# Attention and quantised FFN on one core: the third input chunk split piece by piece, its query chunk in another bank, and the first FFN group turned in fp32 before its scale is known

## What is computed

```python
x = x + xattn(layernorm(x), ctx)       # 8 heads of 64, 77 context rows per batch, 8 batches of 512 rows
x = x + ffn(layernorm(x))

def ffn(x):
    xq = act_fake_quant(x, clip_x)     # scale = sigmoid(clip) * max|x| / 127, over the WHOLE tensor
    gate, up = xq @ wq(w_gate).T, xq @ wq(w_up).T      # 512 -> 1408, weights quantised by row
    h = act_fake_quant(silu(gate) * up, clip_down)     # again one maximum over the whole tensor
    return h @ wq(w_down).T
```

## Time and profile before

| | |
|---|---|
| median of 3 runs | 535.89 us (535.71 to 536.92) |
| profiled execution, its own time | 535.88 us |
| span of its instructions | 534.1 us |
| PE busy | 524.1 us, 98% of the span |
| DVE busy | 449.2 us, 84% |
| ACT busy | 289.8 us, 54% |
| POOL busy | 230.1 us, 43% |
| granted PE clock | full in all 40 slices |

### The profile page before, as it was taken

One profiled execution on the slowest core, in us unless ns is written; L12 is line 12 of the kernel. 1 busy time (PEld: TensorE's weight loads), 2 busy tenths in 40 slices (PEclk: granted clock), 3 DMA queues, 4 the chain that ended last, 5 costly groups with the idle time before them and its releaser, 6 DMA issues.

```text
span 534.1 us, 7958 instructions
## 1 busy us (share of the span) xinstructions
PE 524.1 (98%) x2717; PEld 354.1 (66%) x2724; DVE 449.2 (84%) x812; ACT 289.8 (54%) x417; POOL 230.1 (43%) x349
## 2 busy tenths in 40 slices
PE   8999999999999999999999999999999999999997
PEld 7888688787888888888778644444444445444444
DVE  4966898989989899898899679998999988777663
ACT  4844656565465655554435745545554543999300
POOL 4396679689596876866453000000000000055332
PEclk9999999999999999999999999999999999999999
DMA  8818465846667565435959964942243020499997
GB/s 311 291 79 293 120 167 188 289 150 217 219 201 243 188 226 182 158 110 174 214 88 337 259 187 190 324 118 41 79 119 91 29 39 19 176 334 207 135 111 122
DMA packets 82941, 93.81 MB, mean 176 GB/s; under 512 B 47085, under 2 KB 50157, under 8 KB 82645
## 3 DMA queue, kind: packets, MB, share of 16 engines
q1 hardware_dynamic: 77877, 84.13, 51.2%
q0 software_dynamic: 4320, 7.87, 9.9%
q10 hardware_dynamic: 704, 1.31, 0.8%
HBM read 47.51 MB, written 37.78 MB: 160 GB/s over the span
## 4 chain that ended last, share of the span: by engine, by line
PE 86%; DVE 6%; POOL 2%; DMA 2%; ACT 1%; issue 1%; SPq 0%; DVEq 0%; ACTq 0%; POOLq 0%
PE QO L613 14%; PE SP L618 14%; PE SP L419 6%; PE QO L335 4%; PE QO L333 4%; PE QO L334 4%; PE SP L665 4%; PE PTP L665 4%; PE QO L665 4%; PE PTP L452 3%; PE WOP L490 2%; PE WOP L492 2%; PE WOP L491 2%; PE MI L492 2%; PE MI L490 2%; PE MI L491 2%
## 5 line engine op out<-in xcount | busy, mean ns | idle before, releaser
L1570 POOL DMA_DIRECT2D out<-n2b x30 | 28.0, 975 | 205.6 <-DVE n2b L1389 205.5
L904 ACT ACTIVATE sil<-QO,fsc 128x512 f32<-128x512 f32 x87 | 59.8, 687 | 71.5 <-PE QO L613 70.9
L613 PE MATMUL QO<-nT,wgu 128*128 128x512 bf16 x340 | 87.3, 379 | 0.1
L618 PE MATMUL SP<-nT,wgu 128*128 128x512 bf16 x340 | 87.3, 379 | 0.0
L1332 DVE SCALAR_TENSOR_TENSOR h<-SP,fsc,sil 128x512 f32<-128x512 f32 x87 | 65.3, 750 | 16.7 <-PE SP L618 13.8
L1471 POOL TENSOR_TENSOR PN<-P,rs 128x512 f32<-128x512 f32 x64 | 44.2, 713 | 43.4 <-DVE rs L988 43.4
L1338 DVE TENSOR_REDUCE hmx<-h 128x1 f32<-128x512 f32 (+1 forms) x89 | 60.1, 679 | 2.9
L618 PEld LDWEIGHTS SP<-nT,wgu 128*128 128x128 bf16 x340 | 33.2, 98 | 40.2 <-DVE h L1332 0.3
L613 PEld LDWEIGHTS QO<-nT,wgu 128*128 128x128 bf16 x340 | 33.2, 98 | 40.2 <-ACT sil L904 0.3
L727 ACT ACTIVATE P<-P,r 128x616 f32<-128x616 f32 x32 | 26.0, 811 | 50.0 <-DVE P L979 50.0
L935 ACT ACTIVATE h<-h,g 128x1536 int8<-128x1536 f32 (+2 forms) x38 | 44.3, 1257 | 0.0
(11 more groups left out here) (230 smaller groups left out, 1204.2 us busy)
## 6 DMA issues: line engine op xcount, KB each, us to landing
xTr<-in_xT SPq DMA_DIRECT2D x8, 1024.0 KB, 7.7
xn<-in_x SPq DMA_DIRECT2D x32, 256.0 KB, 4.2
out<-x SPq DMA_DIRECT2D x32, 256.0 KB, 3.1
n_rows<-n SPq DMA_DIRECT2D x32, 256.0 KB, 2.9
n2b<-n_rows SPq DMA_DIRECT2D x32, 256.0 KB, 3.7
out<-n2b POOLq DMA_DIRECT2D x30, 256.0 KB, 5.6
h_spill<-h SPq DMA_DIRECT2D x2, 2816.0 KB, 8.2
h<-h_spill SPq DMA_DIRECT2D x6, 768.0 KB, 6.7
```

What stands on the lines that cost most here:

```text
L613: mm = e.matmul(QO[:, at:at + 512], wgu_v[:, k, cols(ic)], nT[:, b % 2, :, k, :], start=(k == 0), stop=(k == 3))
L618: mm = e.matmul(SP[:, at:at + 512], wgu_v[:, k, cols(NI + ic)], nT[:, b % 2, :, k, :], start=(k == 0), stop=(k == 3))
L904: e.activation(sil[:, n % SR, :], QO[:, (n % 2) * 512:(n % 2) * 512 + 512], ACT.Silu, scale=fsc[:, ic:ic + 1]).then_inc(silu, 1)
```

## The change

It has two named parts and some small ones.

1. **Third chunk.** `load_xT(2)` is issued ahead of five row loads. `split_hi(b, k)` for `k < 3` waits only for the last product that reads piece `k` (`xT_used`). The piece splits of chunk 2 are interleaved on ACT, DVE and POOL with the end of chunk 1; `q_ahead(2)` writes to the bank `MI` and no longer stands in `QO_USES`; `v_rows(4)` goes ahead of `S(4)`.
2. **First FFN group.** Its fp32 rows are turned on PE while the maximum is still being made; each of the four 128-row pieces `k` of the turned rows then goes PSUM -> int8 -> bf16 (`first_chunk`: 0 and 2 on DVE, 1 and 3 on ACT), and `first_two` multiplies 512 columns at a time. `load_n2(0)`, which brings those rows back from memory, is issued one tile earlier; `top_bank` moves the spreading matmul's output.
3. **Around tile 23.** `wo(23)` is cut: three of its four head pairs ahead of `PV_all(6)`, the fourth behind `PT(28)`; `PV_low(6)` goes ahead of `residual(23)`, and `normed(22)` behind `PT_high(28)`. One small step for tile 31 moves from POOL to DVE and one for tile 30 from DVE to POOL.
4. **Small.** `identB` is gone, the last `h_largest` is one reduce instead of two, the last tile is cut 320 / 192 instead of 256 / 256.

```diff
-        QO_USES += [("q", 1, m) for m in range(4)] + [("v", 4), ("q", 2, 0)]
+        QO_USES += [("q", 1, m) for m in range(4)] + [("v", 4)]
...
         def qo_bank(*use):
+            if use == ("q", 2, 0):
+                return MI[:, :]
...
-        LO_POOL = {0: (), 1: (1, 3), 2: (0, 1)}
-        LO_DVE = {0: (0, 1, 2, 3), 1: (0, 2), 2: (2, 3)}
+        LO_POOL = {0: (), 1: (1, 3), 2: (1, 3)}
+        LO_DVE = {0: (0, 1, 2, 3), 1: (0, 2), 2: (0, 2)}
...
+                    if m == 3 and k < 3:
+                        mm.then_inc(xT_used, 1)
...
             PT(2)
+            v_rows(4)
             S(4)
-            v_rows(4)
             PT(3)
...
-            wo(23)
+            w.wait_ge(x1_, 22)
+            wo_pairs(23, PV_ORDER[6][:3], PV_ORDER[6][0], 1).then_inc(wo_most, 1)
             PV_all(6)
             PT(28)
+            wo_pairs(23, PV_ORDER[6][3:], PV_ORDER[6][0], 1).then_inc(wo_mm, 1)
             S(29)
...
-            keep_clock(10)
+            for k in range(4):
+                w.wait_ge(x1_, 31)
+                for tt in range(4):
+                    w.wait_ge(ld_n2b[0][tt], 16)
+                    mm = e.transpose(xT_banks[k][:, cols(tt)], n2b[:, 0, tt, cols(k)], identF[:, :])
+                mm.then_inc(x_tr, 1)
+            keep_clock(3, QO)
             w.wait_ge(g_, G_COL)
...
+            e.matmul(top_bank[0], gcol[:, 0:1].broadcast_to([128, 128]), identF[:, :], start=True, stop=True).then_inc(g_mm, 1)
+            keep_clock(8, QO)
...
+            def first_two():
...
+                for k, ready in ((0, xq_T_dve), (1, xq_T_act)):
+                    w.wait_ge(ready, 1)
+                    for bank, c, _ in four:
+                        e.matmul(bank, wgu_v[:, k, cols(c)], nT[:, 0, :, k, :], start=(k == 0), stop=False)
+                for bank, c, done in four:
+                    w.wait_ge(xq_T_dve, 2)
+                    e.matmul(bank, wgu_v[:, 2, cols(c)], nT[:, 0, :, 2, :], start=False, stop=False)
+                    w.wait_ge(xq_T_act, 2)
+                    e.matmul(bank, wgu_v[:, 3, cols(c)], nT[:, 0, :, 3, :], start=False, stop=True).then_inc(done, 1)
...
             def split_hi(b, k):
                 w.wait_ge(ld_xT, 16 * (b + 1))
-                w.wait_ge(q_mm, 4 * b)
+                if k < 3:
+                    w.wait_ge(xT_used, 3 * (b - 1) + k + 1)
+                else:
+                    w.wait_ge(q_mm, 4 * b)
...
+                    if b == 6 and j != PV_ORDER[6][3]:
+                        w.wait_ge(wo_mm, 23)
+                        w.wait_ge(wo_most, 1)
+                    else:
+                        w.wait_ge(wo_mm, 4 * b)
...
+            def first_chunk(k):
+                w.wait_ge(x_tr, 4)
+                w.wait_ge(g_, G_INV)
+                e.tensor_scalar(xT_i8(k), xT_banks[k], rtop[:, 0:1], k127[:, 0:1], ALU.mult, ALU.mult).then_inc(x_i_dve, 1)
+                w.wait_ge(x_i_dve, k // 2 + 1)
+                e.tensor_copy(nT[:, 0, :, k, :], xT_i8(k).rearrange("p (t c) -> p t c", t=4)).then_inc(xq_T_dve, 1)
...
-                if n == 29:
+                if n == 28:
                     load_n2(0)
```

More of the change, by code:

```diff
@@ L477, in PV_all, with wo_pairs @@
                     PV(b, j)
+            def wo_pairs(n, js, first, last):
+                b, t = n // 4, n % 4
+                for j in js:
+                    w.wait_ge(os_lo, pv_count(b, j) if b == 7 else pv_count(b, 1))
+                    e.matmul(wo_bank(n), os_[:, 0, j, cols(t)], wos[:, 0, j, :], start=(j == first), stop=False)
+                    e.matmul(wo_bank(n), os_[:, 0, j, cols(t)], wos[:, 1, j, :], start=False, stop=False)
+                    mm = e.matmul(wo_bank(n), os_[:, 1, j, cols(t)], wos[:, 0, j, :], start=False, stop=(j == last))
+                return mm
             def wo(n):
-                b, t = n // 4, n % 4
                 w.wait_ge(wo_lo, 1)
+                if n == 1:
+                    w.wait_ge(q_out, 9)
                 if n == 30:
@@ L487, in wo, with keep_clock @@
                     w.wait_ge(x1_, n - 1)
[L488 to L496, removed]
+                wo_pairs(n, range(4), 0, 3).then_inc(wo_mm, 1)
+            def keep_clock(n, bank):
                 for _ in range(n):
-                    e.matmul(WOP[:, 0:128], ones[:, :], ones[:, :], start=True, stop=True)
+                    e.matmul(bank[:, 0:128], ones[:, :], ones[:, :], start=True, stop=True)
             w.wait_ge(const, C_ONES)
@@ L576, in tensor_program @@
             mm.then_inc(sd_mm, 1)
-            keep_clock(10)
-            w.wait_ge(g_, G_COL)
[L579 to L592, removed]
@@ L634, in ffn_last @@
                     mm.then_inc(done, 1)
-            turn(0)
-            turn(1)
-            first_rows(0)
-            turn(2)
-            first_rows(1)
-            turn(3)
-            first_rows(2)
-            first_rows(3)
+            first_two()
             for b in range(NB):
@@ L907, in scalar_program @@
             inverse(0)
[L908 to L911 removed]
+            first_chunk(1)
+            first_chunk(3)
             for b in range(NB):
@@ L1436, in vector_program @@
                     down_out(i, tt)
-            for half in range(2):
-                down_last(half)
+            for i in range(2):
+                down_last(i)
         def gpsimd_program(e):
@@ L1755, in sync_program @@
             e.dma_start(out_v[n], xo[:, 6, :]).then_inc(st_p[0], 16)
-            for half in range(2):
-                ws = slice(256 * half, 256 * half + 256)
-                w.wait_ge(o_a, 2 + half)
+            for i, (_, ws) in enumerate(LAST):
+                w.wait_ge(o_a, 2 + i)
                 e.dma_start(out_v[n + 1][:, ws], xo[:, 7, ws]).then_inc(st_p[1], 16)
```

196 lines of the change are left out of this document (96 added, 100 removed).

## The result

The changed kernel takes 538.34 us (median of 6 runs, 537.05 to 538.92) beside 536.12 us for the kernel before (6 runs): a ratio of 1.0035, 95% interval 1.0023 to 1.0047. I forecast 532.4 us, 530.9 to 534.3. It is **slower by 2.2 us**, on the side to which I had given a chance of 0.02.

What follows compares the result with a forecast made beforehand. PE, busy 98% of the span, was taken to bound the kernel, so time could come only from its standings. Terms of 1.6 + 0.2 + 1.6 + 0.1 = 3.5 us off the 535.89 median gave 532.4 us, range 530.9 to 534.3.

Steps and rivals of the forecast that it cites:

- Chunk 2: At S(4) and PV_rest(0): PE stands 1.75 us, of which 1.6 us is gained; bounds 0.4 and 2.0.
- my high bound: For Chunk 2: 2.0 us gained, if S(9), which stands 0.24 us for DVE's os, gets its share too.
- Around tile 23: Cut of wo(23): at most 0.3 us; 0.2 gained together with Maximum of tile 31; bounds 1.0 gained, 0.2 lost.
- My low bound: For Around tile 23: 0.2 us lost.
- Maximum of tile 31: Small step moved to DVE: the 0.28 us idle goes, gcol ready 0.25 earlier; 0.2 us gained together with Around tile 23.
- The rows of the first group: Loads issued one tile earlier: the last lands near 292.3, thirteen of sixteen transposes wait for it, PE is ready at 294.7.
- my third rival: First group's rows land after 292.3, each us delaying everything: 534.5 us or worse; chance 0.07 for 6 to 8 us, 0.02 above.
- The first group: From the reciprocal to ffn(0, 2): 4.8 us against 6.4, so 1.6 us gained; bounds 1.0 and 1.8.
- Small parts: Single maximum reduce 0.05 us, 320 / 192 cut 0.05, identB and q_copy(2, 0) 0; 0.1 us gained in the sum.
- The 0.02 for slower: Chance that the kernel is slower than before: the first group's rows land later than 295.8, a load of over 8 us.

Runs made afterwards that it cites:

- e1: Changed kernel with only the third input chunk's load put back behind the first weight row's load: 535.24 us, beside 536.28 for the kernel before.
- e10: Kernel before, with only the third input chunk's load moved ahead of the five row loads and first weight row: 538.30 us, beside 536.14 before.
- e3: Changed kernel with the third input chunk's load put back and the part around tile 23 undone: 534.03 us, beside 536.28 for the kernel before.
- e11: Changed kernel with chunk 2, its load and tile 23 as before; first group, maximum of tile 31 and last cut stay: 534.60 us, beside 536.07 before.
- e13: e9 with the first weight row's load ahead of the five row loads, third input chunk behind them: 532.93 us, beside 536.35 for the kernel before.
- e4: e1 with wo(23) still cut and DVE's first three low parts waiting only for its first nine matmuls: 534.76 us, beside 536.28 before.
- e2: Changed kernel with only the part around tile 23 undone, the load left early: 537.28 us, beside 536.28 for the kernel before.
- e5: Changed kernel, load left early, with DVE's, ACT's and POOL's steps on weight row 0 moved later: 536.62 us, beside 536.14 for the kernel before.
- e7: e4 with the four loads of the first group's rows issued earlier on SP: 535.28 us, beside 536.14 for the kernel before.
- e9: e4 with the spreading matmul ahead of the last four transposes and the three operations on ones dropped: 533.68 us, beside 536.07 before.
- e12: e9 with POOL making PN of tile 3 ahead of its first split of chunk 2: 533.53 us, beside 536.07 for the kernel before.

## Why the prediction was wrong, by its steps

- **Chunk 2, 1.6 us expected, 1.6 lost by `S(9)`.** The step of the prediction that failed: "the five row loads and the weight row behind it land about as late as before, since the bytes ahead of the weight row are the same". They are not: `load_xT(2)` stood behind the weight row and now stands ahead, 1 MB more, and the row lands 7.1 us after its issue instead of 5.2 and is read at 52.79 instead of 49.64. DVE already stood 2.51 us for that row, with no slack left, and I had not looked at that wait, because no PE start hung on it before. e1 and e10 price it at 3.3 and 2.2 us (in e10 `PV_rest(0)` stands for the query copy in any case).
- The rest of that term was right in kind. `PV_rest(0)` starts at 62.2 to 63.1 in every kernel whose load is back or whose row-0 steps are late, and I had 62.4. What I had as a single place became three: up to 0.8 us at `PT(3)`, 0.3 to 0.7 at `S(9)`, and in most kernels 0.3 to 0.5 at one of the later `S`. DVE's chain was right: with the load back, low part 3 ends at 61.87 (e3), where I had 61.95. What I had left out is POOL, which makes a split ahead of PN of tile 3. The term by itself is worth 0.8 us (e3 less e11), and 2.0 by `S(9)` with the row loaded early (e13, with another order on SP than the change), which was my high bound.
- **Around tile 23, 0.2 us gained expected, 1.2 lost by the medians and 1.7 by the profiles.** "Three of DVE's four low parts can run from 256.8" failed: the diff shows the relaxed wait in `PV_high` alone, and I read it into `PV_low`. My low bound was 0.2 lost. With the wait supplied (e4), the fourth low part behaves as I said: DVE stands one place later, for 1.30 us, and DVE holds what follows. But then the term is 0.1 us lost and not gained: what PE wins at `S(29)` comes back at `S(30)` and `wo(26)`.
- **Maximum of tile 31.** I had the idle of 0.28 us go and `gcol` ready 0.25 earlier. The idle is 0.21 in e4 and e11, again for POOL's power (`r`), and from tile 31's last statistics to `gcol` DVE takes 1.50 us where it took 1.55: 0.05 gained.
- **The rows of the first group.** In the changed kernel PE stands 0.45 us for them, and 0.3 of it shows between the last `wo` and the spreading matmul (3.81 us against 3.51). That they are the next thing in the way once the stage ahead is faster, my third rival, is what e4 shows: 1.24 us.
- **The first group, 1.6 expected: right.** 1.47 us with the small parts by the medians (e11), 1.52 between the two matmuls in the changed kernel, 4.98 us from the reciprocal to `ffn(0, 2)` where I had 4.8. Reciprocal to `first_two` took 1.53 us where I had 1.3. Timeline of DVE; these rows answer to the earlier trace rows:

```profile
299.65 0.16 DVE L1316 RECIPROCAL clips<-gtop 128x1 f32<-128x1 f32 x1
299.92 0.81 DVE L1332 TENSOR_SCALAR n2b<-WOP,clips,sge 128x512 int8<-128x512 f32 x1
300.77 0.43 DVE L1334 CAST nT<-n2b 128x512 bf16<-128x512 int8 x1
```

  The quantise step out of PSUM takes 0.81 us, 0.26 more than out of SBUF and 0.16 more than I took. The Trainium skill ("VectorE: DVE Perf Modes", section "Why PSUM operands drop a tier") was the better guide than my 0.65, though the ratio here is 1.5 and not 2. Once started, `first_two` has no gap and needs 3.45 us, as forecast.
- **Small parts:** 0.09 us between `ffn(0, 2)` and the second spreading matmul, 0.2 to the end of the execution; I had 0.1.

Two slips in the sums changed nothing: 16 x 0.86 / 4 is 3.44 and not 3.46, and a landing 9.5 us after 287.9 is 5.1 past 292.3, which by rival 3's own rule gives 537.5 and not 537.1.

Of the cases I listed, none had the side right for the right reason. The 0.02 for slower rested on the landing of `n2b`, and what decided was the landing of another load, which a moved line had pushed back.

**What stays open.** With the same order on SP, the first weight row landed after 7.1 and 8.9 us (changed kernel and e2, read at 52.79 and 54.38). No run here shows why. Nor is it shown why the 0.3 to 0.5 us for DVE's `os` turn up at different later `S` in different kernels.

## What to carry to other kernels

When a load moves up a queue, ask of every load that it passes who waits for it first, and how long that engine already stands: here DVE stood 2.5 us for a DMA and had no slack for a later landing, though no PE start hung on it. When a step is cut so that its first part can be overtaken, find every waiter on the old semaphore, on every engine; one that keeps the old count turns the cut into a delay. And a late step on a ring of two buffers is not repaired by using it later, since its next load waits for that use.

## What was not expected of the hardware

A load of 256 KB took 6.9 to 8.9 us to land when 1 MB and five row loads had been issued ahead of it (changed kernel, e2, e5, e10), and 4.6 to 5.6 us behind the five alone (before, e1, e3, e4, e7 to e9, e11, e12). Issued ahead of all of them (e13) it took 5.2 us, so the five row loads cost it nothing that these runs show; what e13 wins is the earlier issue. Issuing the five from SP took 3.81 to 4.19 us behind the 1 MB load and 3.18 to 4.12 without it, so that part of the delay is not clear of its spread. Stores of 256 KB issued right behind four such loads took 5.7 us (e7, median), against 3.1 and 2.9 us, the medians of the two kinds of row stores on the page of the changed kernel:

```profile
out<-x SPq DMA_DIRECT2D x32, 256.0 KB, 3.1
n_rows<-n SPq DMA_DIRECT2D x32, 256.0 KB, 2.9
```
